# One-core attention kernel: context transposes as row halves, the condition in pieces, and parts of steps 0, 1 and 21 to 23 placed one by one

## What is computed

```python
x = x + L0_xcond(ctx, layernorm(x), cond)     # attention: q, k, v from 512 latents and 77 context rows, 16 heads of 64
x = x + L0_ffn(layernorm(x))                  # quantised feed-forward, 128 -> 512 -> 128
for i in range(6):                            # L1_xcond on layernorm(x), its sum added to x at the end
    a = a + attn(adaln(a, cond, n1[i]), rope, 16 heads of 8) @ so[i].T
    a = a + cross_attn(adaln(a, cond, n2[i]), ctx) @ co[i].T
    a = a + gelu(adaln(a, cond, n3[i]) @ f1[i].T + b1) @ f2[i].T + b2
x = x + L1_ffn(layernorm(x))                  # 8 experts, the best one's gate for each row
```

## Time and profile before

| | us |
|---|---|
| median of 3 timed runs (lowest, highest) | 2385.15 (2382.72, 2390.75) |
| the profiled execution | 2395.4 |
| its span, from which all rows are | 2393.6 |
| TensorE busy | 2230.2 (93%) |
| VectorE busy | 1921.1 (80%) |
| ScalarE busy | 1760.9 (74%) |
| GpSimd busy | 1082.9 (45%) |

### The profile page before, as it was taken

How to read it: one execution, slowest core, us unless ns; L and a number is a source line. 1 busy time by engine, 2 the same in 40 slices (tenths; PEclk the granted TensorE clock), 3 DMA queues, 4 the chain that set the end, 5 groups by cost and what they waited for, 6 DMA issues and landing times.

```text
span 2393.6 us, 45707 instructions
## 1 busy us (share of the span) xinstructions
PE 2230.2 (93%) x16778; PEld 969.8 (41%) x16778; DVE 1921.1 (80%) x3983; ACT 1760.9 (74%) x3597; POOL 1082.9 (45%) x1342
## 2 busy tenths in 40 slices
PE   6999999999688999999999999999999999999769
PEld 3455554545322333333333333333343333333336
DVE  6778879697688888888888898888988888886325
ACT  4768778696166778887878887888878788888433
POOL 3556556466334443543354444434344444442213
PEclk9999999999589999999999999999999999999769
DMA  2000000000312321222122322212221222230000
GB/s 83 1 1 1 1 2 1 30 1 19 90 44 68 81 62 49 65 55 65 53 69 63 80 62 66 62 52 77 55 56 53 79 63 64 71 74 24 25 3 18
DMA packets 108568, 113.04 MB, mean 47 GB/s; under 512 B 15809, under 2 KB 96951, under 8 KB 107319
## 3 DMA queue, kind: packets, MB, share of 16 engines
q1 hardware_dynamic: 108345, 110.12, 17.0%
HBM read 14.80 MB, written 1.05 MB: 7 GB/s over the span
## 4 chain that ended last, share of the span: by engine, by line
PE 61%; DVE 15%; ACT 7%; POOL 6%; DMA 5%; issue 3%; SPq 2%; POOLq 0%; DVEq 0%; ACTq 0%
PE psum L1119 10%; DVE A L1609 5%; PE psum L1087 5%; PE psum L1099 5%; PE psum L896 4%; PE psum L1223 4%; PE psum L1231 4%; DMA A<-A 4%; PE psum L979 3%; PE psum L1020 3%; PE psum L1191 3%; DVE A L1631 3%; PE psum L955 2%; PE psum L1180 2%; ACT A L1768 2%
## 5 line engine op out<-in xcount | busy, mean ns | idle before, releaser
L1609 DVE TENSOR_REDUCE A<-psum 128x1 f32<-128x512 f32 x1536 | 967.5, 683 | 127.1 <-PE psum L1099 120.1
L1827 ACT ACTIVATE A<-psum 128x512 f32<-128x512 f32 x1536 | 820.3, 604 | 198.1 <-PE psum L1087 173.4
L1099 PE MATMUL psum<-A 64*128 64x512 bf16 x1536 | 420.1, 391 | 40.6 <-DVE A L1609 17.9
L1087 PE MATMUL psum<-A 64*128 64x512 bf16 x1536 | 405.1, 384 | 6.7 <-DVE A L1609 3.4
L1119 PE MATMUL psum<-A 128*9 128x512 f32 (+1 forms) x3072 | 406.3, 606 | 0.0
L1972 POOL TENSOR_TENSOR A<-A,rden 128x512 f32<-128x512 f32 x256 | 268.8, 1073 | 192.6 <-DVE rden L1494 192.3
L2003 POOL TENSOR_TENSOR A<-A 128x512 f32<-128x512 f32 (+1 forms) x78 | 96.7, 1240 | 299.7 <-DMA A<-A 299.7
L1099 PEld LDWEIGHTS psum<-A 64*128 64x128 bf16 x1536 | 105.4, 94 | 306.7 <-DVE A L1609 130.3
L1857 ACT ACTIVATE A<-psum 77x512 f32<-77x512 f32 x384 | 198.9, 598 | 33.3 <-PE psum L1180 31.5
L1087 PEld LDWEIGHTS psum<-A 64*128 64x128 bf16 x1536 | 104.6, 94 | 266.0 <-DVE A L1609 106.2
L1768 ACT ACTIVATE A<-psum,nm 128x512 f32<-128x512 f32 x256 | 176.1, 688 | 44.4 <-DVE nm L1482 43.8
(11 more groups left out here) (209 smaller groups left out, 3757.6 us busy)
## 6 DMA issues: line engine op xcount, KB each, us to landing
A<-A SPq DMA_DIRECT2D x456, 128.0 KB, 2.4
A<-A SPq DMA_DIRECT2D x336, 64.0 KB, 2.0
A<-zero SPq DMA_DIRECT2D x51, 128.0 KB, 2.3
wl<-in_wl SPq DMA_DIRECT2D x6, 1024.0 KB, 5.9
A<-A SPq DMA_DIRECT2D x36, 78.0 KB, 2.1
A<-in_nT SPq DMA_DIRECT2D x1, 1664.0 KB, 7.0
A<-in_w SPq DMA_DIRECT2D x2, 512.0 KB, 6.9
A<-in_w SPq DMA_DIRECT2D x1, 1024.0 KB, 6.3
```

What stands on the lines that cost most here:

```text
L1087: handle.matmul(bank(b), k_st[bt][lo:lo + ROW, h // 2, k * P:(k + 1) * P], q_st[m % 3][lo:lo + ROW, h // 2, :], start=True, stop=True).the ...
L1099: handle.matmul(bank(b), q_st[m % 3][lo:lo + ROW, pair, q * P:(q + 1) * P], k_st[bt][lo:lo + ROW, pair, :], start=True, stop=True).then_in ...
L1609: handle.tensor_reduce(nm[:, pair // 4, q, j, pair % 4:pair % 4 + 1], bank(BANKS["maximum"][i]), AX.X, ALU.max, negate=True).then_inc(mx, 1)
L1827: handle.activation(pT[:, block % 2, i % GROUP, :], bank(BANKS["scores"][i]), ACT.Exp, scale=HD1 ** -0.5).then_inc(ex, 1)
```

## The change

1. `ctx_turn` is one part for a pair: sixteen transposes of 64 rows into two banks, the lower half of the rows into one, the upper into the other. It signals once for a pair. `ctx_turned` stays two copies on ScalarE of 512 columns each, one for each bank, which puts 64-column runs into their places. `exp` waits on the new count.
2. The condition is cut at columns 2, 6, 16 and 26 (`NORM_PIECES`): piece 0 before the last `out` as before, piece 1 before `qk` 0, pieces 2 and 3 before `v` 0, piece 4 before `maximum` 0. ScalarE's and GpSimd's `gains` are five each. On GpSimd the biases of pieces 0, 1 and 2 stand before `q_thirds` of step 0, the memsets (`constants`) after `k_thirds`. `k_rows` of steps from 1 on, and `other_rows`, wait for all pieces.
3. All places and banks of L0 are new, those of the last batch's feed-forward part and of the experts too.
4. `parts` takes one table of placed parts (`PLACED_*`) in place of the guests: a part listed there is issued before the part that is its key and left out at its steady place. So single parts of steps 0, 1 (some of 2 to 4 behind them) and 20 to 23 stand elsewhere than in the steady order. The steady tables (`TENSOR`, `SCALAR`, `VECTOR`, `POOL`, `SYNC`) and `BANKS` are not changed.
5. In the tail, TensorE has step 22's `cross_max` 5 to 7 behind f1 of step 21 and before its f2; step 23's `cross_max` 0 to 3 before `f_turn` of step 22, number 4 after it and 5 to 7 between its f1 parts; `e_turn` and `e_logits` of step 20 before the cross scores of step 23, four `e_up` of step 20 and one of 21 before the last f2. SyncE's `first_rows` come before `q_swap` of step 0, some `q_zero` a few places later, the experts' weights (`experts`) before `cshift_rows` of step 21.

```diff
+NORM_PIECES = ((0, 2), (2, 6), (6, 16), (16, 26), (26, 36))
-            "ctx_turn": [31, 33, 51, 52, 76, 77, 102, 103, 118, 119, 134, 140, 158, 159, 184, 185],
+            "ctx_turn": [40, 49, 77, 105, 110, 134, 170, 178],
+        PLACED_TENSOR = {
+            ("qk", 0, 0): [("condition", 0, None)],
+            ("v", 0, 0): [("condition", 1, None), ("condition", 2, None)],
+            ("maximum", 0, 0): [("condition", 3, None)],
+            ("maximum", 11, 0): [("b_turn", 0, None)],
...
+            ("cross_max", 5, 22): [("f1", 1, 21), ("f1", 2, 21), ("f1", 3, 21)],
+            ("cross_max", 7, 22): [("weigh", 15, 23)],
+            ("cshift_turn", 0, 22): [("f2", 0, 21)],
...
+            ("cq", 0, 23): [("e_turn", 0, 20)],
+            ("cross_max", 4, 23): [("f_turn", 0, 22)],
+            ("cross_max", 5, 23): [("f1", 0, 22), ("f1", 1, 22)],
+            ("cshift_turn", 0, 23): [("f1", 2, 22), ("f1", 3, 22)],
+            ("cross_scores", 0, 23): [("f2", 0, 22)],
+            ("cross_scores", 2, 23): [("e_logits", 0, 20)],
+            ("catt_turn", 0, 23): [("e_up", 0, 20)],
+            ("f_turn", 0, 23): [("e_up", 1, 20), ("e_up", 2, 20), ("e_up", 3, 20), ("e_turn", 0, 21)],
+            ("f1", 0, 23): [("e_turn2", 0, 20), ("e_logits", 0, 21)],
+            ("f2", 0, 23): [("e_up", 0, 21)],
...
+        PLACED_POOL = {
+            ("q_thirds", 0, 0): [("gains", 0, None), ("gains", 1, None), ("b_power", 0, None), ("gains", 2, None)],
+            ("k_thirds", 0, 0): [("b_power", 1, None)],
+            ("s_norm", 0, 1): [("constants", 0, None)],
...
+        PLACED_SYNC = {
+            ("q_swap", 0, 0): [("first_rows", 0, 0)],
+            ("k_swap", 0, 0): [("q_zero", 0, 0)],
...
-        def parts(table, steps, guests=None, last_ffn=None):
+        def parts(table, steps, guests=None):
             turn = order(table)
+            placed = set(part for at in (guests or {}).values() for part in at)
             backs = [back for _, _, back in turn]
             for p in range(min(backs), steps + max(backs)):
                 for name, i, back in turn:
                     if 0 <= p - back < steps:
-                        for guest in (last_ffn or {}).get((name, i, p - back), ()):
-                            yield guest[0], guest[1], None
                         for guest in (guests or {}).get((name, i, p - back), ()):
-                            yield guest[0], guest[1], STEPS - B + guest[2]
-                        yield name, i, p - back
+                            yield guest
+                        if (name, i, p - back) not in placed:
+                            yield name, i, p - back
...
+                    if m:
+                        sp.wait_ge(prep_ps, 1 + len(NORM_PIECES))
...
                 if name == "ctx_turn":
-                    u, j = divmod(i, 2)
-                    pe.wait_ge(dc, NP0 * bt + u + 1)
-                    b = BANKS0["ctx_turn"][i]
-                    free(b)
-                    for q in range(QT):
-                        t = handle.transpose(psum[0:C, b, q * P:(q + 1) * P], c_p[:, u % 2, j, q, 0:C], ident[:, :])
+                    b, g = BANKS0["ctx_turn"][i], NP0 * bt + i
+                    pe.wait_ge(dc, g + 1)
+                    free(b[0])
+                    free(b[1])
+                    for j in range(2):
+                        for q in range(QT):
+                            for h in range(2):
+                                lo, at = ROW * h, (j * QT + q) * ROW
+                                t = handle.transpose(psum[0:C, b[h], at:at + ROW], c_p[lo:lo + ROW, i % 2, j, q, 0:C],
+                                                     ident[lo:lo + ROW, lo:lo + ROW])
```

More of the change, by code:

```diff
@@ new lines, in build @@
+            "turn": [19, 27, 28, 37, 44, 50, 54, 55, 60, 63, 73, 74, 86, 88, 92, 94, 101, 102, 109, 114, 121, 124, 128, 133, 146,
+                148, 153, 154, 165, 172, 176, 177],
+            "scores": [5, 11, 12, 13, 31, 32, 33, 38, 43, 45, 57, 61, 65, 66, 75, 76, 87, 89, 93, 95, 107, 113, 116, 117, 126, 127,
+                132, 135, 147, 149, 164, 166],
+            "out": [188, 190, 191, 192],
+            "project_c": [-8, 21, 30, 52, 82, 104, 122, 138],
+            "project_k": [-11, 25, 36, 51, 84, 103, 123, 137],
@@ L413, in build @@
+            "ctx_divide": [438, 445, 458, 468, 476, 485, 497, 507],
+            "x_power": 648,
+            "lat_power": 340,
+            "lat_power2": 348,
+            "b_power": [515, 521, 545],
+            "ctx_power": 293,
+            "b_weight": 549,
         }
@@ L611, in build @@
-            "turn": [[5, 7], [0, 5], [7, 4], [7, 6], [6, 0], [2, 6], [5, 6], [2, 7], [7, 0], [5, 0], [7, 2], [2, 1], [6, 5], [6, 5],
-                [0, 6], [6, 5], [2, 0], [5, 3], [5, 4], [6, 7], [2, 0], [0, 1], [7, 4], [4, 7], [6, 5], [5, 7], [7, 0], [6, 1], [6,
-                4], [6, 2], [4, 3], [7, 5]],
-            "ctx_turn": [6, 5, 7, 4, 5, 0, 6, 0, 7, 4, 6, 5, 5, 7, 0, 6],
-            "weigh": [7, 6, 7, 7, 6, 4, 7, 5],
-            "out": [3],
+            "condition": [1, 3, 5, 1, 5],
@@ L617, in build @@
+            "turn": [[1, 2], [6, 4], [5, 3], [6, 7], [7, 3], [2, 7], [3, 7], [6, 5], [4, 3], [4, 3], [1, 3], [6, 2], [5, 0], [0, 6],
+                [5, 6], [0, 3], [1, 4], [0, 2], [4, 6], [6, 5], [2, 1], [7, 0], [7, 4], [4, 6], [7, 6], [6, 5], [1, 0], [2, 7], [1,
+                0], [4, 3], [1, 0], [4, 2]],
+            "ctx_turn": [[0, 1], [6, 1], [3, 6], [4, 6], [7, 5], [7, 5], [5, 2], [3, 5]],
+            "weigh": [0, 7, 7, 7, 6, 4, 7, 6],
+            "out": [6],
             "b_turn": [4],
-            "b_up": [6, 6, 1, 7],
+            "b_up": [2, 7, 1, 0],
@@ L904, in weight_sums, with condition @@
                 owner[b] = (ready, 3)
-            def condition(lo, hi):
-                if lo:
+            def condition(i):
+                lo, hi = NORM_PIECES[i]
+                if i:
                     pe.wait_ge(in_late, 128)
-                b = BANKS0["condition"][0 if lo else 1]
+                b = BANKS0["condition"][i]
                 free(b)
                 for j in range(lo, hi):
-                    t = handle.matmul(psum[:, b, j * B:(j + 1) * B], nT[:, j * D:(j + 1) * D], condT[:, :], start=True, stop=True)
+                    t = handle.matmul(psum[:, b, (j - lo) * B:(j + 1 - lo) * B], nT[:, j * D:(j + 1) * D], condT[:, :], start=True, stop=True)
                 t.then_inc(prep_ps, 1)
-                owner[b] = (gains, 3 if lo else 1)
+                owner[b] = (g_copied, i + 1)
             def part0(name, i, bt):
@@ L1318, in passes @@
             def passes():
-                for name, i, m in parts(TENSOR, STEPS, EXPERTS_TENSOR, FFN_TENSOR):
+                for name, i, m in parts(TENSOR, STEPS, PLACED_TENSOR):
                     if m is None:
@@ L1724, in passes @@
             def passes():
-                for name, i, m in parts(VECTOR, STEPS, EXPERTS_VECTOR, FFN_VECTOR):
+                for name, i, m in parts(VECTOR, STEPS, PLACED_VECTOR):
                     if m is None:
@@ L1919, in passes @@
             def passes():
-                for name, i, m in parts(SCALAR, STEPS, EXPERTS_SCALAR, FFN_SCALAR):
+                for name, i, m in parts(SCALAR, STEPS, PLACED_SCALAR):
                     if m is None:
@@ L2066, in passes @@
             def passes():
-                for name, i, m in parts(POOL, STEPS, EXPERTS_POOL, FFN_POOL):
+                for name, i, m in parts(POOL, STEPS, PLACED_POOL):
                     if m is None:
```

716 lines of the change are left out of this document (519 added, 197 removed), and 8 rows, old and new, of tables (EXPERTS_POOL, PLACED_POOL).

## The result

| | us |
|---|---|
| median before, same chip (4 runs) | 2387.28 (2382.72 to 2390.75) |
| median after (4 runs) | 2367.24 (2365.67 to 2367.46) |
| ratio, 95% interval | 0.9912 (0.9897 to 0.9928) |
| predicted | 2342, range 2318 to 2366 |
| profiled execution after, its span | 2367.46, 2365.3 |

The kernel is faster by 20 us where 43 were forecast; the time is 1.2 us above the range.

The account below looks back on a forecast made before the run. TensorE's work was taken to bound L0 and the steady steps, waiting chains the transition and tail. Context transposes 14, transition 6, steps 0 and 1 2, tail 21 sum to 43 us: 2385.15 - 43 = 2342 us, range 2318 to 2366.

Parts of the forecast that it names:

- Context transposes: First block's attention (L0): half transposes save 0.48 us a pair, 15.4 over 32, taken as 14 us (0 to 20).
- Rival 2: Context transposes bring nothing, by a fixed cost per small instruction or ScalarE's copies setting the pace; 2356 us, chance 0.15.
- Transition: Between L0 and step 0's first maximum: condition in pieces and earlier first rows start the maxima 6 us earlier (0 to 9.4).
- Steps 0 and 1: Singly placed parts at the start of the layer steps only trim gaps: 2 us gained, between 3 lost and 9 won.
- Steady steps: Steps 2 to 20, order and banks unchanged: nothing gained but what they inherit from their ends.
- Steps 21 to 23: The tail with the experts: four edits to its order, together 21 us gained.
- (b): Step 23's cross maxima put ahead of and among feed-forward parts: turn of the shifts 8 us earlier (4 to 12).
- (c): Experts: five e_up parts and two smaller ones moved ahead of the last f2, 8 us gained (4 to 10).
- rival (1): L0's gaps shrink too and the clock stays up in parts of the tail: some 20 us more, 2322; chance 0.13.
- (3): Tail gives back its gain: half of its 21 us and the ramp's 2 lost, about 2355 us; chance 0.12.
- (5): Slower: context turns in L0 waiting for two banks idle TensorE once a pair; 2406 us at 2 us a pair; chance 0.05.
- The base: Starting time: the timed median lies 10.25 us under the profiled execution's 2395.4, so 43 us is subtracted from 2385.15.

Follow-up runs that it names:

- e3: The changed kernel with whole context transposes (eight of 128 rows a pair) instead of halves; 2371.87 us, ratio 0.9945.
- e4: The kernel before with only the context transposes as halves (sixteen of 64 rows a pair), all orders kept; 2388.15 us, ratio 1.0015.
- e8: The changed kernel with the condition in two pieces as before, the rest of the transition kept; 2369.73 us, ratio 0.9910.
- e13: e5 with the row halves of the maximum parts exchanged on TensorE and VectorE, no part moved; 2383.44 us, ratio 0.9973.
- e5: The changed kernel with steps 0 to 4 back in the steady order on TensorE, ScalarE, VectorE and GpSimd; 2353.46 us, ratio 0.9851.
- e11: e5 with the maximum, scores, weigh and exp parts and reductions of steps 20 to 23 also in the steady order; 2359.48 us, ratio 0.9874.
- e12: e11 with two neighbours swapped in TensorE's steady order, leaving 6 unpaired row-half matmuls a step instead of 10; 2359.46 us, ratio 0.9871.
- e15: e5 run again, on the same chip as e14; 2354.15 us, ratio 0.9868.
- e2: The changed kernel with everything placed from step 18 on, experts and their banks included, put back as before; 2380.61 us, ratio 0.9979.
- e7: The changed kernel with only the experts placed anew in the tail, other parts of steps 18 to 23 steady; 2376.19 us, ratio 0.9937.
- e1: The changed kernel with steps 0 to 4 back in the steady order on TensorE, ScalarE and VectorE, not GpSimd; 2363.88 us, ratio 0.9916.
- e14: The changed kernel itself timed again, on another chip; 2359.40 us, ratio 0.9885.

## Why the prediction was wrong

**Context transposes: 14 forecast, 8 measured.** The order was right, the term was mis-sized twice. The price of a pair as halves, which I took from the score transposes as 0.67 us, is 0.78. The group of the changed kernel in L0:

```profile
L1368 PE MATMUL psum<-ident,A 64*77 64x64 f32 x512 | 24.9, 233 | 4.0 <-POOL A L2346 2.5 <-ACT A L2137 0.9 <-issue 0.5
```

24.9 / 32 = 0.78, so 12.0 us of work were won, not 15.4. And I let all of it but a tenth count, because VectorE and ScalarE have room on average; e3 and e4 show that a third of it, or all of it in the old order, turns into idle time. Room of other engines over a batch says nothing about the waits of each pair. Rival 2, no gain at all, is not what happened: e3, with whole transposes, loses 8 us. The Trainium skill's page "TensorEngine Tiling (Array Packing)", section Instruction Overhead, by my reading of it would leave the work as it was; this case's trace does not agree, the rows show a third of it gone (24.9 us where 36.9 were).

**Transition: 6 forecast, 7.2 measured.** Held in size, and e8 shows that the pieces do it; the chain was another. Shifted by L0's 7.9 us I had the thirds of q at 607.6 and the maxima at 621.6; the thirds began at 604.0 and the first maximum at 617.94. The key rows that I had last came 3.7 us sooner than I said, and VectorE, forecast for 622.1, sets the end, at 621.15 (timeline of VectorE after):

```profile
614.42 4.69 DVE L1945 TENSOR_SCALAR A<-A,small 128x128 f32<-128x128 f32 x4
...
619.95 0.87 DVE L1962 BATCH_NORM_STATS2 A<-x_st 128x6 f32<-128x128 f32 x4
...
621.15 2.45 DVE L1977 TENSOR_REDUCE A<-psum 128x1 f32<-128x512 f32 x4
```

**Steps 0 and 1: 2 gained forecast, 8.1 lost.** This is the step that failed most, 10 of the 15 us between the 43 and the 28.3 of the spans (the context transposes are 6, the tail 3): "this trims gaps and no more", with 3 us as the worst. I looked at VectorE's gaps, as it is the busier engine there, and did not ask what a single place does to the neighbours on TensorE. They part row halves that would run together, and spread them over more stretches; e13 shows in the steady steps that parting costs, and the records of the ramp show 23 more lone starts than before's. The single places account for some 4.5 us of the 8.1 (e5, e11, e12 and e15 against the others); the rest is open. VectorE's waits for a maximum in the ramp grew, 21.2 us before, 19.6 in e5, and after:

```profile
DVE A L1977 <- PE psum L1467: 25.3, 33, 2.1
```

**Steady steps: nothing.** Right; the 3.4 us of the table are before's profile (e4, with the same order, has 1118.3 us where the change has 1119.0).

**Steps 21 to 23: 21 forecast, 13 to 16 by e2** (17.9 against before's profile). (b) held: from the first cross maximum of step 23 to the turn of the shifts it took 2292.91 - 2269.74 = 23.2 us, and 12.7 after (10.5 less, 8 forecast). TensorE after:

```profile
2264.60 0.70 PE L1531 MATMUL psum<-A 64*128 64x77 bf16 x16 [3.29 <-DMA A<-A]
...
2277.30 0.40 PE L1541 MATMUL psum<-ident,A 128*128 128x128 bf16 x4
...
2281.74 0.41 PE L1548 MATMUL psum<-A 64*77 64x512 bf16 x2
```

But these cross maxima began 270.4 us behind the first maximum of step 21 instead of 265.1: the parts put ahead of them cost 5 us, and I had counted moved work as free. (c) gave 6 net instead of 8, with 11.5 behind the last f2 and 5.8 paid ahead. The stretch behind it came to 46.2 us; I had said 49 to 50. The clock is not separable here: from 2236 to 2336 us it is 0.80 where it was 0.59, and over the tails of before, e2, e7, after and e8 the time at the lower level falls from 82 to 72, 62, 41 and 22 us while the tail falls from 389.0 to 385.1, 379.0, 371.1 and 364.3. e8 has the change's tail orders and is 6.8 us shorter than after, so some of this is the clock alone. It may be most: the seven profiles with the change's tail (after, e1, e3, e5, e8, e14, e15) run from 22 us at the lower level and 364.3 us to 44 and 373.2, some 0.37 us of time for each us. By that line, drawn out to more low time than they have, the 31 us between e2 and the change are worth 11 of its 14 us. This is an estimate, and the orders may themselves be what keeps the clock up, since they leave TensorE less idle; no run holds the clock still. My sum took its times from rows at before's clock and had no term for a clock that rises; only rival (1) named it.

**Rivals.** (3), the tail gives back and the ramp loses, was nearest in mechanism; its price for the ramp was 2 us and the ramp lost 8. (1), the clock stays up in the tail, came true in its condition (0.80 for 0.59) without its 20 us more. (5), waits for two banks in L0: e4's L0 is 1.9 us longer, but only 1.3 us of the idle time ahead of its context transposes ends at ScalarE, and 0.9 in the change.

**The base.** I took the profiled execution's 10.25 us over the median off at the end and kept the sum. Its surplus lay in the stages that I compared rows in, some 4 us each in the steady steps and the tail, as e4 shows, and not outside them.

That the measured time lies only 1.2 us above the range is partly luck of the timing: on the chip of e14 the same kernel lies inside it, and the terms are as wrong there.

## What to carry to other kernels

Where half-array matmuls run in pairs, the order of neighbours is a cost of its own: before a single part is moved, count how many pairs it parts and how many stretches it makes. Here work taken off the fullest engine gave time only together with an order made for it, and then two thirds of it; test both edits alone, as each may show nothing. A start won ahead of a stage with waits between engines is not yet a gain: look where the next fixed event, four steps on, stands.

## What the runs showed of the hardware

Two bf16 matmuls of 64 rows and 512 columns in different halves start 3 to 7 ns apart; one of the same half follows 0.21 to 0.23 us later. One more that starts by itself cost 0.17 us of TensorE's work in e13.

Eight fp32 transposes of 128 rows with 77 columns took 1.15 us (34.7 / 32 = 1.08 in e3's order); sixteen of 64 rows, in two halves and two banks, 0.78. Those with 128 columns took 0.67, so fewer columns cost more here; why is open.

By the clock records of the traces, TensorE's clock fell to its lower level 3 to 7 us behind the last out of L0 in every profile, when TensorE had begun to wait, and rose again 32 to 35 us behind the first reduction of step 0, wherever that stood (at 668.0 in before, 655.4 after, 654.6 in e5, 662.1 in e8). Only in e1, where TensorE waited 10.5 us in that step, it was 42 us (661.1).
